# Graph attention on one core: start and tail in halves, another order, and row transposes of 1 MB in place of 512 KB

## The reference

```
h     = relu(layernorm(x))                      # (64, 128, 512) float32
out   = h @ weight ; q = h @ wq ; k = h @ wk    # 512 x 512 weights
alpha = q @ k^T                                 # (64, 128, 128)
alpha = softmax(max(alpha, 0) * (adj != 0), axis=1)
x + alpha @ out
```

## Time and profile before

| | us |
|---|---|
| median of 3 runs | 415.78 |
| lowest and highest run | 415.6, 416.57 |
| the profiled execution | 416.35 |
| its span | 414.6 |

### The profile page before, as it was taken

How to read it: one execution, slowest core, us unless ns; L and a number is a source line. 1 busy time by engine, 2 the same in 40 slices (tenths; PEclk the granted TensorE clock), 3 DMA queues, 4 the chain that set the end, 5 groups by cost and what they waited for, 6 DMA issues and landing times.

```text
span 414.6 us, 9426 instructions
## 1 busy us (share of the span) xinstructions
PE 404.2 (98%) x3571; PEld 320.8 (77%) x3571; DVE 296.5 (72%) x572; ACT 277.5 (67%) x589; POOL 259.7 (63%) x275
## 2 busy tenths in 40 slices
PE   5999999999999999999999999999999999999996
PEld 4444544879798797979889797979889797979983
DVE  4787689696767777686777678676777768656466
ACT  4489696486777776776767776677767677653523
POOL 0279887969486775939587685939577594920000
PEclk9999999999999999999999999999999999999999
DMA  8953758996969798896978699996988689393022
GB/s 285 370 106 75 207 101 203 224 222 175 188 199 199 243 127 215 203 216 173 194 240 149 167 209 227 186 196 205 169 250 167 166 209 233 40 183 115 2 102 103
DMA packets 161465, 75.03 MB, mean 181 GB/s; under 512 B 135312, under 2 KB 143504, under 8 KB 161424
## 3 DMA queue, kind: packets, MB, share of 16 engines
q1 hardware_dynamic: 160848, 73.42, 76.8%
q10 hardware_dynamic: 576, 1.05, 0.7%
HBM read 24.12 MB, written 16.78 MB: 99 GB/s over the span
## 4 chain that ended last, share of the span: by engine, by line
PE 80%; POOL 6%; DVE 5%; ACT 4%; DMA 3%; issue 1%; SPq 1%; DVEq 0%; ACTq 0%; POOLq 0%
PE bank L1063 10%; PE bank L1065 10%; PE bank L1066 10%; PE bank L1081 9%; PE bank L1080 9%; PE bank L1078 9%; PE s_bank L1094 3%; PE s_bank L1093 3%; PE s_bank L1092 3%; DMA x_sb<-in_x 2%; POOL hn_lo L387 2%; PE bank L1099 2%; PE bank L1100 2%; PE bank L1101 2%; ACT exps L585 1%
## 5 line engine op out<-in xcount | busy, mean ns | idle before, releaser
L387 POOL TENSOR_TENSOR hn_lo<-h,hn_hi 128x512 f16<-128x512 f32 x64 | 74.6, 1177 | 54.9 <-ACT hn_hi L503 54.8
L493 ACT ACTIVATE h<-x_sb,shift,rstd 128x512 f32<-128x512 f32 x64 | 49.8, 803 | 24.6 <-POOL shift L382 24.6
L413 POOL TENSOR_TENSOR hn_lo<-s,hn_hi 128x512 f16<-128x512 f32 x56 | 63.5, 1167 | 0.3 <-ACT hn_hi L508 0.3
L1065 PE MATMUL bank<-hT_lo,mt_hi 128*128 128x256 f16 x224 | 61.1, 273 | 0.0
L1066 PE MATMUL bank<-hT_hi,mt_lo 128*128 128x256 f16 x224 | 61.1, 273 | 0.0
L1063 PE MATMUL bank<-hT_hi,mt_hi 128*128 128x256 f16 x224 | 61.1, 273 | 0.0
L1078 PE MATMUL bank<-wt_hi,hT_hi 128*128 128x256 f16 x224 | 61.1, 273 | 0.0
L1081 PE MATMUL bank<-wt_hi,hT_lo 128*128 128x256 f16 x224 | 61.1, 273 | 0.0
L1080 PE MATMUL bank<-wt_lo,hT_hi 128*128 128x256 f16 x224 | 61.1, 273 | 0.0
L508 ACT ACTIVATE hn_hi<-s 128x512 f16<-128x512 f32 x56 | 33.7, 625 | 28.0 <-POOL s L402 22.1
L1063 PE MATMUL bank<-hT_hi,m_hi 128*128 128x256 f16 x168 | 45.8, 273 | 0.6 <-ACT bank L527 0.5
(11 more groups left out here) (140 smaller groups left out, 1091.2 us busy)
## 6 DMA issues: line engine op xcount, KB each, us to landing
x_sb<-in_x SPq DMA_DIRECT2D x16, 1024.0 KB, 5.6
out_h<-x_sb SPq DMA_DIRECT2D x64, 256.0 KB, 2.1
adj_sb<-in_adj SPq DMA_DIRECT2D x16, 256.0 KB, 5.3
w_sb<-in_L_gnn_weight SPq DMA_DIRECT2D x1, 1024.0 KB, 11.4
hn_lo<-in_L_gnn_wk ACTq DMA_DIRECT2D x2, 256.0 KB, 3.8
hn_lo<-in_L_gnn_wk SPq DMA_DIRECT2D x2, 256.0 KB, 3.6
hn_hi<-in_L_gnn_wq SPq DMA_DIRECT2D x2, 256.0 KB, 6.4
hn_hi<-in_L_gnn_wq ACTq DMA_DIRECT2D x2, 256.0 KB, 6.7
```

The costliest lines, as they stand in the source:

```text
L387: nc.gpsimd.tensor_tensor(hn_lo[:, s, b], h[:, b], hn_hi[:, s, b], ALU.subtract).then_inc(h_split, 1)
L413: nc.gpsimd.tensor_tensor(low, s32[:, f], high, ALU.subtract).then_inc(s_split, 1)
L493: nc.scalar.activation(h[:, b], x_sb[:, s, b], ACT.Relu, bias=shift[:, b:b + 1], scale=rstd[:, b:b + 1]).then_inc(h_made, 1)
L1065: nc.tensor.matmul(o, bh[:, k, cols], al[:, :, k], start=False, stop=False, skip_group_check=True)
```

## The change

The edits, in the order of the kernel's time:

1. x of group 0 and w are loaded in halves with a semaphore each; statistics and scales of group 0 are taken by halves (stats_first, first_scales), as is the maximum over w. The counts of rstd_made, ln_step, w_maxed and x_loaded[0] shift accordingly.
2. PE makes twelve transposes of the identity (WARM) ahead of the first real one. The transposes of wq are laid between halves of product_m(0) and product_m(1).
3. On DVE the statistics of group 1 stand later, those of group 3 between the pieces of T of group 1, and mask, mt, v and wt pieces are in another order. On ACT exponentials(0) stand behind two copies of h, hi_of_h(3, 1, 0) one step earlier, hi_of_whole_v(1, 3) ahead of the sums.
4. PE's three waits ahead of period 2 (v_split, mt_split, wt_split in full) become waits for the pieces, ahead of the product that first reads each.
5. The four row transposes of a group become two: transpose_all waits for the scores of two groups before, for the fourth hi of the sums, transposes hi of rows and sums (1 MB), waits for the fourth lo, and transposes lo. sT_landed goes. Group 1, which has no sums, still has 512 KB each.
6. In the last group lo_of_p is made in two pairs around v_lo(1), and the last graph's output, residual and store are made in two halves of the columns.

```diff
+            for b in (0, HG):
+                sp.dma_start(x_sb[:, 0, b:b + HG], x_dram[:, b:b + HG, :]).then_inc(x0_loaded[b // HG], 16)
+            for k in (0, HK):
+                sp.dma_start(w_sb[:, k:k + HK], weight.rearrange("(k p) d -> p k d", p=N)[:, k:k + HK]).then_inc(w_loaded[k // HK], 16)
...
-            def transpose_sums(g):
+                transpose_part(hT_lo, hn_lo, g % 2, GB, hT_landed)
+
+            def transpose_all(g):
+
+                sp.wait_ge(scores_filled, g - 1)
                 sp.wait_ge(s_hi_made, sums(g, 4))
-                transpose_part(hT_hi, hn_hi, g % 2, GB, sT_landed)
+                transpose_part(hT_hi, hn_hi, g % 2, 2 * GB, hT_landed)
                 sp.wait_ge(s_split, sums(g, 4))
-                transpose_part(hT_lo, hn_lo, g % 2, GB, sT_landed)
+                transpose_part(hT_lo, hn_lo, g % 2, 2 * GB, hT_landed)
...
+            def first_scales(f):
+
+                c = slice(HG * f, HG * (f + 1))
+                pool.wait_ge(meanvar_made, HG * (f + 1))
...
             normalise_h(2, 2, 3)
-            exponentials(0)
             act.wait_ge(hT0_landed[2], 2 * 16)
             hi_of_h(2, 0, 2)
             hi_of_h(2, 0, 3)
+            exponentials(0)
...
             lo_of_whole_t(1, 0)
-            lo_of_wt(3)
-            for b in range(GB):
-                stats_all(3, 3, b)
             lo_of_whole_t(1, 1)
+            stats_all(3, 3, 0)
+            stats_all(3, 3, 1)
             lo_of_whole_t(1, 2)
+            stats_all(3, 3, 2)
+            stats_all(3, 3, 3)
             lo_of_whole_t(1, 3)
             for b in range(GB):
                 residual(0, 0, b)
+            make_mask(2, 0, 2)
             lo_of_mt(0)
+            lo_of_whole_v(1, 0)
             lo_of_mt(1)
-            lo_of_whole_v(1, 0)
+            lo_of_whole_v(1, 1)
+            lo_of_wt(3)
+            lo_of_whole_v(1, 2)
             lo_of_mt(2)
+            lo_of_whole_v(1, 3)
             lo_of_mt(3)
...
-            lo_of_p(LAST)
+            lo_of_p(LAST, range(HG))
             lo_of_v(LAST, 1, bank[VE][:], 0, 1)
+            lo_of_p(LAST, range(HG, GB))
...
+            for k in range(WARM):
+                nc.tensor.transpose(top_bank[:, N * (k % K):N * (k % K + 1)], ident[:], ident[:])
             for r in range(K):
                 transpose_wk(r)
+
             transpose_wq(0)
+            product_m(0, range(2))
             transpose_wq(1)
-            product_m(0)
+            product_m(0, range(2, K))
             transpose_wq(2)
+            product_m(1, range(2))
             transpose_wq(3)
-            product_m(1)
+            product_m(1, range(2, K))
...
+            for f in range(2):
+                dst, cols = last_half[f], slice(HD * f, HD * (f + 1))
+                nc.tensor.matmul(dst, p_hi[:, b], v_hi[:, b, cols], start=True, stop=False)
```

More of the change, by code:

```diff
@@ L184, in out_bank @@
             return [bank[FREE][:], s_flat, bank[TA][:], bank[FREE][:]]
+        last_half = [bank[FREE][:, :HD], s_flat[:, :HD]]
         wT_bank = [bank[VB][:].rearrange("p (k n) -> p k n", k=K), bank[VE][:].rearrange("p (k n) -> p k n", k=K)]
         top_bank = bank[FREE]
+        x0_loaded = [sem(f"x0_loaded{k}") for k in range(2)]
         x_loaded = [sem(f"x_loaded{s}") for s in range(UNROLL)]
@@ L191, in graph_attention_kernel @@
         stored = [sem(f"stored{s}") for s in range(UNROLL)]
-        w_loaded = sem("w_loaded")
+        w_loaded = [sem(f"w_loaded{k}") for k in range(2)]
         wq_loaded = [sem(f"wq_loaded{r}") for r in range(K)]
@@ L526, in copy_p1_t @@
                 act.wait_ge(t_split, 4 * g)
+                if isinstance(g, int) and g == FIRST:
+                    act.wait_ge(v_split, GB + TB + 1)
                 nc.scalar.activation(bank[TB][:], bank[TA][:], ACT.Copy).then_inc(t_copied, 1)
@@ L616, in hi_of_h2 @@
                 def hi_of_h2(b):
[L617 removed]
+                    hi_of_h(g + 2, j % 2, b, turn(i, j))
                 copy_p1_t(g)
@@ L841, in softmax_sum, with lo_of_p @@
                 nc.vector.reciprocal(row_inv[:], row_sum_s[:]).then_inc(inv_made, 1)
-            def lo_of_p(g):
-                for b in range(GB):
+            def lo_of_p(g, graphs=range(GB)):
+                for b in graphs:
                     vec.wait_ge(p_hi_made, GB * g + b + 1)
@@ L964, in _ @@
                                            pow2[:, 2:3], ALU.mult, ALU.mult).then_inc(scale_step, 1)
-            stats_all(1, 1, 2)
-            stats_all(1, 1, 3)
+            for b in range(1, GB):
+                stats_all(1, 1, b)
             vec.wait_ge(scale_step, 6)
@@ L1120, in period @@
                 pe.wait_ge(hT_landed[s], 2 * 16 * turn(i, j))
+                if g == FIRST:
+                    pe.wait_ge(v_split, GB + TA + 1)
                 product_t(s, N_P1, bank[TA][:], True)
-                pe.wait_ge(sT_landed[s], 2 * 16 * sum_turn(i, j))
+                if g == FIRST:
+                    pe.wait_ge(v_split, GB + TE + 1)
+                first_use(g, mt_split, T1)
                 product_t(s, N_P5, bank[TE][:], True)
@@ L1126, in period @@
                 product_v(s, N_P1, bank[VA][:], True)
+                first_use(g, wt_split, T1)
                 product_v(s, N_P5, bank[VE][:], True)
@@ L1130, in period @@
                 product_t(s, N_P2, bank[TA][:], False)
+                first_use(g, mt_split, T2)
                 product_t(s, N_P6, bank[TB][:], False)
@@ L1134, in period @@
                 product_v(s, N_P2, bank[VA][:], False)
+                first_use(g, wt_split, T2)
                 product_v(s, N_P6, bank[VB][:], False)
@@ L1138, in period @@
                 pe.wait_ge(t_summed, done(g, 1))
+                first_use(g, mt_split, T3)
                 product_t(s, N_P7, bank[TB][:], False)
                 pe.wait_ge(v_summed, done(g, 1))
+                first_use(g, wt_split, T3)
                 product_v(s, N_P7, bank[VB][:], False)
@@ L1145, in period @@
                 pe.wait_ge(t_summed, done(g, 2))
+                first_use(g, mt_split, T4)
                 product_t(s, N_P4, bank[TB][:], False)
@@ L1149, in period @@
                 pe.wait_ge(v_summed, done(g, 2))
+                first_use(g, wt_split, T4)
                 product_v(s, N_P4, bank[VB][:], False)
@@ L1296, in _ @@
                 pe.wait_ge(v_split, GB * LAST + (2 if b < HG else 4))
-                product_out(LAST, b)
+                if b < GB - 1:
+                    product_out(LAST, b)
+            for f in range(2):
+                dst, cols = last_half[f], slice(HD * f, HD * (f + 1))
+                nc.tensor.matmul(dst, p_hi[:, b], v_hi[:, b, cols], start=True, stop=False)
+                nc.tensor.matmul(dst, p_hi[:, b], v_lo[:, b, cols], start=False, stop=False)
+                nc.tensor.matmul(dst, p_lo[:, b], v_hi[:, b, cols], start=False, stop=True).then_inc(out_filled, 1)
 _INS = ["x", "adj", "L0_gnn_weight", "L0_gnn_wq", "L0_gnn_wk"]
```

100 lines of the change are left out of this document (55 added, 45 removed).

## The result

The changed kernel takes 417.0 us (median of 22 runs, 416.29 to 419.05) against 416.5 us for the kernel before in the same comparison (22 runs, 415.6 to 416.84): a ratio of 1.0019, 95% interval 1.0011 to 1.0027. The interval leaves out 1, so this is a small loss, inside the 0.3% that the prediction calls no change; the forecast was a gain of 1.7 us. The profiled execution took 417.04 us with a span of 415.2, against 416.35 and 414.6 before, so these two traces are 0.7 us apart and can be laid side by side.

What follows compares the result with a forecast made beforehand. PE, busy 98% of the span, was taken as the bound. Gains of 1.6 us (start and period 2) and 0.4 (tail), less 0.3 (x of group 4), made 1.7: 415.78 to 414.1 us, range 412.4 to 416.4.

Steps and rivals of the forecast that it cites:

- rival B: Period 2: group 2's lo 1 to 3 us late for PE, or group 4's x for DVE; 415.4 us; chance 0.24.
- part 5: Two 1 MB transposes per group: hidden in steady periods, x of group 4 just in time; price 0.3 us.
- part 6: Tail: v_lo(1) earlier, last residual and store halved; net gain 0.4 us, bounds 0 and 0.8.
- The bound: PE is busy 98%; only the start, period 2 and the tail can win, steady periods of 23.58 us cannot.
- Part 1: Start: loads in halves, warm transposes, interleaved products of M; gain 0.1 us, bounds 0 and 0.77.
- Parts 2 and 3: Group 0's rows earlier, gain 0.28 us; DVE and ACT order in 50 to 76, gains 0.44, 0.10 and 0.31.
- Part 4: Period 2: POOL 1.6 us earlier (bounds 0.8 and 2.9), so PE goes on 1.6 us earlier than before.
- The landing of 1 MB: A 1 MB transpose lands after 7.2 us, bounds 4.3 and 13.4; group 2's lo at 72.4, 2 us of cover.

Runs made afterwards that it cites:

- e5_unweave: Kernel after, with the wq transposes again in pairs ahead of the products instead of woven between their halves: 416.24 us, ratio 0.9999.
- e10_act: Kernel after with four 512 KB transposes, old tail, wq in pairs, and two ACT copies of group 3's sums moved behind period 2's copies: 413.36 us, ratio 0.9930.
- e1_four: Kernel after, with four row transposes of 512 KB in each group again, rows first: 414.98 us, ratio 0.9972.
- e3_g2: Kernel after, with group 2 alone in four 512 KB transposes and later groups in two of 1 MB: 415.4 us, ratio 0.9977.
- e4_tail: Kernel after, with the tail of the kernel before: 416.71 us, ratio 1.0008.
- e9_hold: e1_four, with only the load of x for group 4 held back on SP's queue: 418.5 us, ratio 1.0045.

## Why the prediction was wrong

It was wrong: 414.1 forecast, 417.0 measured, above the range's 416.4. Of these 2.9 us some 0.7 are the starting point: the forecast counts from the 415.78 us of three runs, and 22 runs gave 416.5 for the kernel before. The rest is a gain of 1.7 us forecast and a loss of 0.5 to 0.8 measured. The mechanism that happened is rival B's, mainly in the half that it names second (x of group 4 late against DVE); but B still counted a gain of 0.4, and 417.0 lies above B's 416.6 as well. The step that failed is the price of part 5; besides it, part 6 had the wrong sign. Step by step:

- **The bound.** Right. All gains and losses lie in the start, in period 2 and in the tail, and steady periods did not move: lo was issued at 107.24 and landed at 114.9, some ten us ahead of its use.
- **Part 1.** A gain of 0.1 was taken, and the first product of group 0 came 0.13 us later (25.24 for 25.11). The sum 9.24 + 16 x 0.43 + 12 x 0.11 gives 17.7 with the measured start of 9.50, and the trace has 17.76. The maximum over w ended early enough, as forecast, and that four transposes move onto PE's path was named. But the comparison was made with the wrong thing: what counts is not whether PE meets the maximum over w in time, it is what PE could have done without weaving. e5_unweave shows 0.38 us given away. The loads in halves were not taken out by themselves; the 7.75 us against 8.32 in e5_unweave are the sign of their gain.
- **Parts 2 and 3.** Right in effect. None of PE's waits of the earlier trace rows at 30, 64 and 75 is left. Part 2 had its reason too large: the last small transpose of group 0 was issued at 25.39 and not near 23, 0.6 us earlier than before, which was enough for the 0.28. Period 2 started at 74.78, not 74.4: 0.23 of the difference because the first product of group 0 was at 25.24 and not at 25.0, and 0.15 for the lo transpose, which landed at 74.8.
- **Part 4.** Right in kind, short in size. ACT's copy of the fourth sum, which again waits for POOL, started at 79.26 instead of 80.37, 1.1 us earlier where 1.6 was taken (bounds 0.8 to 2.9). PE's wait behind it went from 0.63 to 0.40. e10_act shows that what was left of this chain was worth 1.1 us. ACT's row in the kernel after:

```profile
79.26 0.63 ACT L527 ACTIVATE hn_hi<-s 128x512 f16<-128x512 f32 x1 [0.71 <-POOL s L426]
```

- **Part 5, the step that failed.** The place, the queue and the waiting instruction were named, and the price taken was 0.3 us. Measured it is 1.5 in the traces (26.31 us from the scores of group 1 to those of group 2 in the kernel after, 24.81 in e1_four) and 1.7 to 2.0 in the times of e3_g2 and e1_four. Terms of that sum: hi was issued at 61.49, not 61.0 (0.5). The issues took 4.8 and 4.9 us and not 4.2 (1.5 for both, with the gaps between). From the stores to x it took 5.7 and not 4.9 us (0.8): the four stores landed after 3.1 us in the median and 4.1 at most, against 2.8 and 2.9 before, while lo was still under way until 74.8; that this is the reason isn't shown. The load took 5.7 and not 5.4 (0.3). That is 3.0 us: x landed at 82.7 instead of 79.7. The exponentials were done at 82.3, 0.5 later than the forecast's 81.8. With 1.2 us of statistics ahead of the sum, DVE had to have x by 81.1, a slack of 1.4, so the sum of the softmax came 1.6 us late (83.92). The issue and the load stayed inside their bounds, and the other two terms had been given none. All erred to the same side, for they aren't independent: a longer transpose delays the next one and with it the stores and the load. The prediction even had the sentence "with an issue of 4.9 us it is 0.6 late", and stopped there, without adding that the start of hi and the stores could slip too. Under all of these terms lies that the rows' transposes no longer go out while SP is idle, but behind the fourth sum.
- **The landing of 1 MB.** Taken as 7.2 us; by line in the kernel after (ns min/median/max of the issue, then landings; one of each 15 is group 1's of 512 KB), and then the landing of lo of group 2 alone:

```profile
L291 SPq DMA_TRANSPOSE hT_hi<-hn_hi x15: 1317/4835/5700, 36.5 to 361.6; - x15
L291 SPq DMA_TRANSPOSE hT_lo<-hn_lo x15: 3120/4970/5692, 38.3 to 367.1; - x15
...
DMA to landing us min/median/max: 4.3/6.9/9.1
...
DMA to landing us min/median/max: 8.4/8.4/8.4
```

  Right in the median, and 1.2 us too short for the one that counts. lo of group 2 landed at 74.8 and not at 72.4: the 2 us of cover that the prediction counted against PE's 74.4 were used up, and PE lost 0.15 us. That it was no more is luck. The upper bounds were drawn from the line of hT_hi alone (issues up to 3.7 us); the line of hT_lo, which the earlier trace rows doesn't show, goes up to 4.1.
- **Part 6.** Wrong in sign: +0.4 taken, 0.28 lost in the trace, and e4_tail gives some of it back. The prediction itself said that DVE has the same work before v_lo(3), which makes the tail DVE's; then a split of p_lo and of the residual can only add to it. The prediction priced the last residual at 0.4 us for half the columns; the two halves took 0.47 each, one behind the other, and both are DVE's. The bounds (0 to 0.8) left out a loss, and gave no reason for it. The last store of 128 KB landed in 2.0 us, like one of 256 KB before, so nothing came from there.

The sum as it came out in the two traces: 0.88 at the start of period 2, -1.25 in it, -0.28 in the tail, together -0.65 us, where +1.7 stood. With the three losing edits left out and one cause of the old stalls removed, the same idea gives 413.0 to 413.4 us, 0.7% less than before.

## What to carry to other kernels

Merging two transfers lets the whole wait for the later part's data; ask what the issuing queue did in the time in which the earlier part used to go out. A transfer that is hidden from its consumer can still be late for others: count how long its issue holds the queue, and follow every DMA that stands behind it to its own consumer, in the first iterations separately from the steady state, because there the slack is smallest. When several durations in one chain are estimated, carry the pessimistic end through the whole chain once, rather than pricing one term at a time. Splitting the last operation in two helps only where the engine that makes it is idle in between; look first for an idle time in the rows of the tail.

## What the runs showed of the hardware

- An issue of a DMA transpose holds SP's queue the longer the larger it is: 2.44 us median for 512 KB, 4.8 to 5.0 for 1 MB, up to 5.7. One of 1 MB saved no queue time over two of 512 KB, and the median landing went from 4.8 to 6.9 us. The Trainium skill (DMA: Bandwidth & Descriptors, "Issuing engines are not separate DMA queues") calls the time that an engine needs to initiate a DMA usually small relative to the DMA; the traces don't agree for transposes, where it is 4.8 of 6.9 us. For the plain load of x, 1 MB as well, they do: 0.39 of 5.7 us.
- A single wait of 2.44 us ahead of a matmul was followed by 3.6 us at the 1.2 GHz level (granted clock 0.54) in the trace of e9_hold; three of its five executions show the lower mean clock and took 0.9 us more than the other two. The wait of 1.17 us in the trace of the kernel after was followed by no fall.
- The granted clock of the page reads 1.00 in the first microseconds of every trace here, while PE's first transposes run at half speed: the twelve warm ones of the kernel after take 418 ns each, those of wk in the kernel before 421 ns. Behind the warm ones most of wk's take 273 ns.
